# Four-head layer: scores in four row groups and banks, masks added by VectorE, keys in one copy, no loop

## The chip, the cores and the metric

One core of a Trainium2 chip (trn2) runs the kernel. Times are device microseconds of one execution, the median of the runs of a kernel; the profile and its rows come from one profiled execution. The tensor engine is called TensorE or PE, the vector engine VectorE or DVE, the activation engine ScalarE or ACT, the general one GpSimd or POOL.

## The reference, cut to what matters

Four transformer layers follow each other on x of 16 x 256 tokens of 128 features. The change is in the third ("layer 2", counted from 0), whose attention has four heads of 32 features, and a feed-forward part beside it:

```python
q_in = x @ Wq.T
qkv = (q_in @ Wqkv.T + bqkv).reshape(Bs, Ls, 3, Ds)       # q, k, v: G = 4 heads, dh = 32
scores = einsum('blgd,bmgd->bglm', q, k) * scale
h = relu(q_in) @ Wop.T
dx = sigmoid(h @ W2.T + b2) * Ls                          # one reach per token
dx_g = dx[:, None, :, :] + windows[None, :, None, None]   # windows 32, 64, 128, 256
win_mask = where(idx[None, :] < idx[:, None], BIG, dist)
masked = where(win_mask > dx_g, -BIG, scores)
attn = softmax(masked + scores)
out = einsum('bglm,bmgd->blgd', attn, v)
# beside it, on the same normed x
h = silu(x @ w1 * w1_s) * (x @ w2 * w2_s)                 # 512 wide
h = gelu(h @ h1 * h1_s); h = gelu(h @ h2 * h2_s)          # 512 x 512 twice
y = h @ w3 * w3_s
```

Both results are added to x.

## The kernel before, in words

Layer 2 (`layer2`) works in eight passes (`PASSES = 8`) over two sequences each, 512 tokens. Each engine has a hardware loop (`Fori`) of its own over the passes; between them stand semaphores (`sig(...)`), whose values a loop works out in registers. An engine executes its list in order, so the order written in `pe_`, `act_`, `dve_` and `pool_` is the order of the work. Two sequences of a pass are the blocks p = 0 and 1.

TensorE, in this order: the queries' input (bank 4), `up` (the gated first stage of the feed-forward, banks 6, 7 and 0, 1), the reach (bank 5), q, v and k (bank 4 in turn); `mid(0, 0)` and `mid(1, 0)` for the first two chunks; `scores(0)`; the rest of `mid(0..3, 0)`, which is the first 512 x 512 stage in three products per chunk; `turn()`, the transposes of the next pass's normed x into bank 4; `scores(1)`; `turned(0, g)`, the transposes of the softmax weights of block 0, laced with the second 512 x 512 stage `mid(c, 1)`; `values(0)`; `turned(1, g)`; `wide_out`, `values(1)` and the sum in bank 2. Where the columns of a line say 128*128 they are rows and columns of the loaded weights.

`scores(p)` before: three bf16 products of the identity with the masks put the masks into banks 0, 1 and 2 (L1733, L1734), then three f32 products over all 128 rows add the scores (L1736, L1737). For this the keys lie in `kb`, a copy for each head with zeros in the other heads' rows; ScalarE writes the four copies (L1853), and GpSimd has cleared the whole array once.

VectorE, in order: relu (L1959), `gated(c)` (L1949), q's copy, the reach, `split` of h into high and low parts (L1941, L1943, signal `f_h`), `masks(0)`, two more splits, `masks(1)`, `stats` (L1901), `maxima(0)` (L1982, L1983, three reductions with the sign turned), the norm of the next pass, `sums(0)`, the splits of the gelus (signal `f_sp`) for chunks 0 and 1, `maxima(1)`, `turned_out(0, 1)` (L1993, the copies of the transposed weights), splits of chunks 2 and 3, further copies, the final addition (L2012).

ScalarE, in order: q_in's copy (L1840), the reach's exp (L1842), `silu(0..3)` (L1836) with v's copy between, the keys, `exps(0)` (L1860, L1863, eight exps with row sums), four `gelu` (L1869, signal `f_ig`), the copy of the turned x (L1877), `exps(1)`, `head_out(0)` (L1887), four gelus, `head_out(1)`. A function of another table costs an ACT_TABLE_LOAD ahead of it.

GpSimd multiplies the weights by the reciprocal sums (L2028, L2029).

In layer 1, a loopless part of the same kernel, VectorE already adds masks and takes maxima in one instruction (`tensor_tensor_reduce`, L1483 and L1484, shown as CUSTOM_DVE_ANT_0), and ScalarE takes the exps of its result (L1373, L1374). In layer 0 four row groups of TensorE give scores into four banks (L793).

Of the kernel before, what the change touches and what calls it, by code (L numbers as in the profile page):

```python
# [68 lines left out]
def program(nc, ins, out):  # L69
# [3 lines left out]
    with ctx:  # L73
# [1562 lines left out]
        def layer2():  # L1636
# [4 lines left out]
            kb = carve(G2, 512)  # L1641
# [18 lines left out]
            PRE = 8  # L1660
            ORDER = ["in", "q", "v", "k", "t"]
# [6 lines left out]
            MID_BANKS = ((6, 7, 5, 3), (6, 7, 0, 1))  # L1668
# [8 lines left out]
            def pe_(pe):  # L1677
# [10 lines left out]
                pe.wait_ge(pre_k, 2)  # L1688
                pe.wait_ge(pre, 4)
                with pe.Fori(0, PASSES) as i:  # L1690
# [13 lines left out]
                    def mid(c, layer, parts=range(C2)):  # L1704
# [3 lines left out]
                        if parts[0] == 0:  # L1708
                            pe.wait_ge(pre, PRE)
                            if layer == 0 and c == 0:  # L1710
                                pe.wait_ge(f_h.s, f_h.at(i, 1))
                            if layer == 0 and c == 2:
                                pe.wait_ge(ot.s, ot.at(i, -1))
                                pe.wait_ge(d_e.s, d_e.at(i, 0))
                            if layer == 0 and c == 3:
                                pe.wait_ge(t_e.s, t_e.at(i, -1))
                            if layer == 1 and c == 2:
                                pe.wait_ge(s_ex.s, s_ex.at(i, 1))
# [21 lines left out]
                    def turned(p, g):  # L1740
# [7 lines left out]
                        for c, src in enumerate((pr0[p][:, g, 128:256], pr1[p][:, g, :], pr0[p][:, g, 0:128])):  # L1748
                            mm = pe.transpose(PS[(3, 4)[n % 2]][:, c * 128:(c + 1) * 128], src, ident)
                        mm.then_inc(t_f.s, 1)  # L1750

                    def values(p):
                        pe.wait_ge(t_e.s, t_e.at(i, 4 * p + G2 - 1))
                        pe.wait_ge(ot.s, ot.at(i, p - 1))
                        for g in range(G2):
                            r = slice(DH2 * g, DH2 * (g + 1))
                            pe.matmul(PS[5][r, 0:256], v_sb[:, 2 * p + 1, r], pt[g][:, 0:256], start=True, stop=False, skip_group_check=True)
                        for g in range(G2):
                            r = slice(DH2 * g, DH2 * (g + 1))
                            pe.matmul(PS[5][r, 0:128], v_sb[:, 2 * p, r], pt[g][:, 256:384], start=False, stop=True,  # L1760
# [13 lines left out]
                    pe.wait_ge(ot.s, ot.at(i, -1))  # L1774
# [22 lines left out]
                    mid(3, 0)  # L1797
                    pe.wait_ge(ln_x.s, ln_x.at(i, 0))
# [29 lines left out]
            def act_(act):  # L1828
                act.wait_ge(m_f.s, m_f.before(0))
                act.activation(xnT, PS[4][:, :], ACT.Copy).then_inc(m_e.s, 1)  # L1830
                act.wait_ge(pre_k, 2)
                with act.Fori(0, PASSES) as i:
# [18 lines left out]
                    for g in range(G2):  # L1851
                        r = slice(DH2 * g, DH2 * (g + 1))
                        ins_ = act.activation(kb[r, g, :], PS[4][r, :], ACT.Identity, bias=L["bk"][r, :])  # L1853
                    ins_.then_inc(m_e.s, 1)

                    def exps(p):
                        act.wait_ge(s_mx.s, s_mx.at(i, p))
                        act.wait_ge(t_f.s, t_f.at(i, 4 * p + 3 - 8))
                        for g in range(G2):
                            act.activation(pr0[p][:, g, :], PS[g // 2][:, g % 2 * 256:(g % 2 + 1) * 256], ACT.Exp, bias=nmx[:, p, 0, g:g + 1],  # L1860
                                           accum_out=sm[:, p, 0, g:g + 1])
                        for g in range(G2):
                            ins_ = act.activation(pr1[p][:, g, :], PS[2][:, g * 128:(g + 1) * 128], ACT.Exp, bias=nmx[:, p, 1, g:g + 1],  # L1863
# [21 lines left out]
            def head_out(act, i, p):  # L1885
                act.wait_ge(pv.s, pv.at(i, 4 * p + 3))
                act.activation(oT[:, p * 256:(p + 1) * 256], PS[5][:, 0:256], ACT.Identity, bias=L["bv"]).then_inc(ot.s, 1)  # L1887

            def dve_(dve):
# [45 lines left out]
                with dve.Fori(0, PASSES) as i:  # L1935
# [9 lines left out]
                    def gated(c):  # L1945
                        dve.wait_ge(f_s.s, f_s.at(i, c))
# [42 lines left out]
                    def turned_out(*which):  # L1989
                        for n in which:  # L1990
                            dve.wait_ge(t_f.s, t_f.at(i, n))
                            dve.wait_ge(pv.s, pv.at(i, n - G2))
                            dve.tensor_copy(pt[n % G2], PS[(3, 4)[n % 2]][:, 0:384]).then_inc(t_e.s, 1)  # L1993
# [21 lines left out]
            def pool_(pool):  # L2015
                pool.memset(kb, 0.0).then_inc(pre_k, 1)
# [5 lines left out]
                with pool.Fori(0, PASSES) as i:  # L2022
# [139 lines left out]
```

## Time and profile before

| | |
|---|---|
| median of 3 runs | 2264.98 us (2264.29 to 2267.79) |
| the profiled execution | 2265.04 us |
| its span | 2263.2 us |
| the passes of layer 2 | about 1277 to 1699 us of the span |
| PE busy | 2043.8 us |
| DVE busy | 1461.5 us |
| ACT busy | 1159.4 us |
| POOL busy | 895.9 us |

Matmuls are pipelined: one starts before the last has ended, so the distance between starts is the cost of one in a row, and the length printed is longer. In a timeline row the first number is the start, the second the time covered; in brackets is the idle time of that engine before it and what ended it. PEclk is the share of the full TensorE clock that was granted, 1.00 for 2.4 GHz and 0.50 for 1.2 GHz.

### The profile page before, as it was taken

To read this page: it belongs to the slowest core of one execution; us is meant where nothing else is said; L and a number is where in the kernel's file an instruction comes from. 1 tells how busy PE (TensorE), PEld (TensorE's weight loads), DVE (VectorE), ACT (ScalarE), POOL (GpSimd) and SP (SyncE) were. 2 spreads that over 40 slices of the span, in tenths; PEclk is the share of its full clock that TensorE was granted. 3 is DMA by queue.
4 is the path that set the end of the run, shared out by engine and by line. 5 is a ranking of instruction groups with operands and counts; after the bars stand their busy time and mean duration, and the time that the engine had idled before them with its cause. 6 is when DMAs were issued, how large, how long until landed. Compare 5 with 4: busy or idle time off the path is not lost.

```text
span 2263.2 us, 47747 instructions
## 1 busy us (share of the span) xinstructions
PE 2043.8 (90%) x15692; PEld 1546.9 (68%) x15692; DVE 1461.5 (65%) x5301; ACT 1159.4 (51%) x3600; POOL 895.9 (40%) x1416
## 2 busy tenths in 40 slices
PE   5887977399999999999999899999997999999998
PEld 2555644277777777777777566666665777777776
DVE  6999843366666666666666655555556777777776
ACT  3443342155455555555554455555545666666665
POOL 3113255345455444444444411111114545454554
PEclk9887779689999999999999899999998999999999
DMA  6000016600000000000000000000000000000001
GB/s 190 8 1 1 8 34 159 173 2 1 2 2 1 1 2 1 2 2 1 2 2 1 1 0 0 0 0 0 0 0 1 2 2 2 2 2 1 2 1 39
DMA packets 37479, 36.86 MB, mean 16 GB/s; under 512 B 5648, under 2 KB 34448, under 8 KB 36368
## 3 DMA queue, kind: packets, MB, share of 16 engines
q1 hardware_dynamic: 31632, 29.82, 4.2%
q0 software_dynamic: 5632, 4.33, 1.4%
q8 instruction: 116, 1.90, 0.3%
q14 instruction: 99, 0.81, 0.1%
HBM read 23.53 MB, written 10.62 MB: 15 GB/s over the span
## 4 chain that ended last, share of the span: by engine, by line
PE 67%; issue 11%; DVE 8%; ACT 8%; POOL 4%; DMA 1%; DVEq 0%; SPq 0%; another core or an unknown queue 0%; POOLq 0%; ACTq 0%
PE bank L1313 7%; PE bank L1302 6%; PE bank L1241 5%; PE bank L1288 4%; PE bank L1285 4%; PE bank L1335 4%; PE bank L1226 2%; PE bank L1228 2%; PE bank L1227 2%; ACT work L1373 2%; PE bank L1700 2%; PE bank L1722 2%; PE bank L1305 2%; PE bank L1234 2%; PE bank L1724 2%
## 5 line engine op out<-in xcount | busy, mean ns | idle before, releaser
L1596 POOL TENSOR_TENSOR work<-work 128x128 f32<-128x128 f32 (+1 forms) x1048 | 503.6, 512 | 698.5 <-DVE work L1496 698.5
L1373 ACT ACTIVATE work<-work 128x128 f32<-128x128 f32 x524 | 206.7, 395 | 546.0 <-DVE work L1484 546.0
L1491 DVE COPY work<-bank 128x384 f32<-128x384 f32 x520 | 283.6, 550 | 26.5 <-PE bank L1313 11.1
L1374 ACT ACTIVATE work<-work 128x256 f32<-128x256 f32 x524 | 258.6, 493 | 0.0
L1313 PE MATMUL bank<-w_const,work 128*128 128x128 f32 x1560 | 228.9, 283 | 1.0 <-POOL work L1596 1.0
L1484 DVE CUSTOM_DVE_ANT_0 work<-bank,mask 128x256 f32<-128x256 f32 x524 | 220.0, 420 | 0.0
L1313 PEld LDWEIGHTS bank<-w_const,work 128*128 128x128 f32 x1560 | 166.9, 141 | 47.5 <-issue 43.1
L1517 DVE COPY work<-bank 128x512 f32<-128x512 f32 x136 | 93.5, 687 | 158.7 <-PE bank L1236 152.1
L1483 DVE CUSTOM_DVE_ANT_0 work<-bank,mask 128x128 f32<-128x128 f32 x524 | 151.0, 288 | 53.6 <-PE bank L1288 49.1
L1302 PE MATMUL bank<-work 128*64 128x256 f32 x1032 | 171.7, 410 | 4.4 <-DVE work L1517 4.0
L1226 PE MATMUL bank<-l_xn_hi,l_qk_hi 128*128 128x256 f32 x532 | 163.6, 308 | 2.9 <-DVE l_xn_lo L1437 2.8
L1288 PE MATMUL bank<-work 64*128 64x256 f32 x1048 | 163.5, 390 | 0.0
L1392 ACT ACTIVATE work<-bank 128x512 f32<-128x512 f32 x266 | 154.4, 580 | 9.0 <-PE bank L1228 8.4
L1228 PE MATMUL bank<-l_xn_hi,l_qk_lo 128*128 128x256 f32 x532 | 151.3, 284 | 0.0
L1227 PE MATMUL bank<-l_xn_lo,l_qk_hi 128*128 128x256 f32 x532 | 150.7, 283 | 0.0
L1335 PE MATMUL bank<-w_l,work 128*128 128x128 f32 x1024 | 134.8, 275 | 0.0
L1609 POOL TENSOR_TENSOR work<-work 128x512 f32<-128x512 f32 x129 | 134.3, 1041 | 0.0
L1285 PE MATMUL bank<-work 64*128 64x128 f32 x1048 | 133.1, 332 | 0.0
L1335 PEld LDWEIGHTS bank<-w_l,work 128*128 128x128 f32 x1024 | 125.0, 191 | 0.0
L1285 PEld LDWEIGHTS bank<-work 64*128 64x128 f32 x1048 | 81.7, 191 | 62.9 <-issue 49.9
L1496 DVE RECIPROCAL work<-work 128x2 f32<-128x2 f32 x524 | 84.9, 162 | 54.5 <-ACT work L1374 52.4
L1302 PEld LDWEIGHTS bank<-work 128*64 128x64 f32 x1032 | 53.5, 137 | 95.3 <-issue 95.3
(338 smaller groups left out, 4934.2 us busy)
## 6 DMA issues: line engine op xcount, KB each, us to landing
w_l<-in_l SPq DMA_DIRECT2D x1, 3210.5 KB, 10.4
w_l<-in_l SPq DMA_DIRECT2D x2, 1540.0 KB
w_f<-in_f SPq DMA_DIRECT2D x1, 3072.0 KB, 13.9
x_sb<-in_x SPq DMA_DIRECT2D x4, 512.0 KB, 6.0
normed_rows<-work SPq DMA_DIRECT2D x1, 2048.0 KB, 9.3
even_experts<-x_sb SPq DMA_DIRECT2D x8, 256.0 KB, 3.6
residual<-x_sb SPq DMA_DIRECT2D x1, 2048.0 KB, 9.7
qk<-in_qk SPq DMA_DIRECT2D x2, 1024.0 KB
```

The lines of the kernel that those rows point to most:

```text
L1226: pe.matmul(to, qk_hi[:, n, ws], x, start=True, stop=False)
L1228: mm = pe.matmul(to, qk_lo[:, n, ws], x, start=False, stop=True)
L1285: pe.matmul(scored(i, 2 * j + n)[:, Q0], q[r, 0:128], q[r, 256:384], start=True, stop=True, skip_group_check=True)
L1288: pe.matmul(scored(i, 2 * j + n)[:, Q1], q[r, 128:256], q[r, 256:512], start=True, stop=True, skip_group_check=True).then_inc(s_f.s, 1)
L1302: pe.matmul(PS[5][r, 0:256], v[:, 0, h], pt[(2 * j + n) % 4][:, 0:256], start=True, stop=False, skip_group_check=True)
L1313: mm = pe.transpose(PS[2 + g % 2][:, to * 128:(to + 1) * 128], pr[g % 4][:, c * 128:(c + 1) * 128], ident)
L1335: mm = pe.matmul(PS[7][:, t * 128:(t + 1) * 128], h2[u % 2][:, c * 256 + t * 128:c * 256 + (t + 1) * 128], L["down"][:, (2 * e + c) * D:(2 ...
L1373: act.activation(pr[g % 4][:, Q0], pr[g % 4][:, Q0], ACT.Exp, scale=-1.0, bias=nmx[:, g % 4, 0:1], accum_out=sm[:, g % 4, 0:1])
L1374: act.activation(pr[g % 4][:, Q1], pr[g % 4][:, Q1], ACT.Exp, scale=-1.0, bias=nmx[:, g % 4, 1:2], accum_out=sm[:, g % 4, 1:2]).then_inc(s ...
L1484: dve.tensor_tensor_reduce(pr[g % 4][:, Q1], scored(i, g)[:, Q1], mask[:, Q1], -1.0, BIG, ALU.add, ALU.min, nmx[:, g % 4, 1:2]).then_inc(s ...
L1491: dve.tensor_copy(pt[g % 4], PS[2 + g % 2][:, 0:384]).then_inc(s_te.s, 1)
L1596: ins = pool.tensor_tensor(w, w, spread(rc[:, g % 4, q:q + 1], w.shape[1]), ALU.mult)
```

## The change

Scores of a head come from its own 32 rows of `qT` and `kT`, as eight products, four with 256 and four with 128 columns, each head into a bank of its own (0 to 3). The keys are one array `kT` with one copy, and the clearing of the old one is gone. The mask products are gone; VectorE adds the bf16 masks while it takes the maxima, writes the masked scores (with the sign turned) to SBUF, and ScalarE takes the exps from there. The banks are dealt anew: `mid(2, 0)` and `mid(3, 0)` use banks 4 and 5, the turned weights 5 and 4, the values bank 3. The waits follow: `turn()` waits for the third gelu of the stage, since its bank 4 is now read by it; `scores` waits for the maxima of the last block. The four `Fori` are Python loops, so that the eight passes stand one after the other in the program.

```diff
-            MID_BANKS = ((6, 7, 5, 3), (6, 7, 0, 1))
+            MID_BANKS = ((6, 7, 4, 5), (6, 7, 0, 1))
+            TURN_BANKS = (5, 4)
...
-                with pe.Fori(0, PASSES) as i:
+                for i in range(PASSES):
...
                             if layer == 0 and c == 2:
-                                pe.wait_ge(ot.s, ot.at(i, -1))
+                                pe.wait_ge(m_e.s, m_e.at(i, place["k"]))
+                            if layer == 0 and c == 3:
                                 pe.wait_ge(d_e.s, d_e.at(i, 0))
-                            if layer == 0 and c == 3:
                                 pe.wait_ge(t_e.s, t_e.at(i, -1))
                             if layer == 1 and c == 2:
-                                pe.wait_ge(s_ex.s, s_ex.at(i, 1))
+                                pe.wait_ge(s_mx.s, s_mx.at(i, 1))
...
                     def scores(p):
-                        pe.wait_ge(mb_s.s, mb_s.at(i, p))
-                        pe.wait_ge(s_ex.s, s_ex.at(i, p - 1))
-                        pe.wait_ge(o_e.s, o_e.at(i, -1))
-                        for j in range(2):
-                            pe.matmul(PS[j][:, :], ident16[:, :], mb0[p][:, 2 * j:2 * j + 2, :].rearrange("p g k -> p (g k)"), start=True, stop=False)
-                        pe.matmul(PS[2][:, :], ident16[:, :], mb1[p].rearrange("p g k -> p (g k)"), start=True, stop=False)
-                        for j in range(2):
-                            pe.matmul(PS[j][:, :], qT[:, p * 256:p * 256 + 128], kb[:, 2 * j:2 * j + 2, p * 256:(p + 1) * 256], start=False, stop=True)
-                        pe.matmul(PS[2][:, :], qT[:, p * 256 + 128:(p + 1) * 256], kb[:, :, p * 256 + 128:(p + 1) * 256],
-                                  start=False, stop=True).then_inc(s_f.s, 1)
+                        pe.wait_ge(s_mx.s, s_mx.at(i, p - 1))
+                        if p == 0:
+                            pe.wait_ge(dv.s, dv.at(i, GATED_3))
+                            pe.wait_ge(o_e.s, o_e.at(i, -1))
+                            pe.wait_ge(ot.s, ot.at(i, -1))
+                        for g in range(G2):
+                            r = slice(DH2 * g, DH2 * (g + 1))
+                            pe.matmul(PS[g][:, 0:256], qT[r, p * 256:p * 256 + 128], kT[r, p * 256:(p + 1) * 256], start=True, stop=True, skip_group_check=True)
+                        for g in range(G2):
+                            r = slice(DH2 * g, DH2 * (g + 1))
+                            mm = pe.matmul(PS[g][:, 256:384], qT[r, p * 256 + 128:(p + 1) * 256], kT[r, p * 256 + 128:(p + 1) * 256],
+                                           start=True, stop=True, skip_group_check=True)
+                        mm.then_inc(s_f.s, 1)
...
                     mid(3, 0)
+                    pe.wait_ge(f_ig.s, f_ig.at(i, 2))
                     pe.wait_ge(ln_x.s, ln_x.at(i, 0))
                     turn()
                     scores(1)
...
-                    for g in range(G2):
-                        r = slice(DH2 * g, DH2 * (g + 1))
-                        ins_ = act.activation(kb[r, g, :], PS[4][r, :], ACT.Identity, bias=L["bk"][r, :])
-                    ins_.then_inc(m_e.s, 1)
+                    act.activation(kT, PS[4][:, :], ACT.Identity, bias=L["bk"]).then_inc(m_e.s, 1)

                     def exps(p):
                         act.wait_ge(s_mx.s, s_mx.at(i, p))
-                        act.wait_ge(t_f.s, t_f.at(i, 4 * p + 3 - 8))
                         for g in range(G2):
-                            act.activation(pr0[p][:, g, :], PS[g // 2][:, g % 2 * 256:(g % 2 + 1) * 256], ACT.Exp, bias=nmx[:, p, 0, g:g + 1],
+                            act.activation(pr0[p][:, g, :], pr0[p][:, g, :], ACT.Exp, scale=-1.0, bias=nmx[:, p, 0, g:g + 1],
                                            accum_out=sm[:, p, 0, g:g + 1])
-                        for g in range(G2):
-                            ins_ = act.activation(pr1[p][:, g, :], PS[2][:, g * 128:(g + 1) * 128], ACT.Exp, bias=nmx[:, p, 1, g:g + 1],
+                            ins_ = act.activation(pr1[p][:, g, :], pr1[p][:, g, :], ACT.Exp, scale=-1.0, bias=nmx[:, p, 1, g:g + 1],
...
                     def maxima(p):
+                        dve.wait_ge(mb_s.s, mb_s.at(i, p))
                         dve.wait_ge(s_f.s, s_f.at(i, p))
-                        for j in range(2):
-                            dve.tensor_reduce(nmx[:, p, 0, 2 * j:2 * j + 2], PS[j][:, :].rearrange("p (g k) -> p g k", k=256), AX, ALU.max, negate=True)
-                        dve.tensor_reduce(nmx[:, p, 1, :], PS[2][:, :].rearrange("p (g k) -> p g k", k=128), AX, ALU.max, negate=True).then_inc(s_mx.s, 1)
+                        dve.wait_ge(t_f.s, t_f.at(i, 4 * p + 3 - 8))
+                        for g in range(G2):
+                            dve.tensor_tensor_reduce(pr0[p][:, g, :], PS[g][:, 0:256], mb0[p][:, g, :], -1.0, BIG, ALU.add, ALU.min, nmx[:, p, 0, g:g + 1])
+                            ins_ = dve.tensor_tensor_reduce(pr1[p][:, g, :], PS[g][:, 256:384], mb1[p][:, g, :], -1.0, BIG, ALU.add, ALU.min,
+                                                            nmx[:, p, 1, g:g + 1])
+                        ins_.then_inc(s_mx.s, 1)
...
-                pool.memset(kb, 0.0).then_inc(pre_k, 1)
```

## Rows read from the trace of the kernel before

**Rows 1.** The page, busy time: engine, us, share of the span, instructions.

```profile
PE 2043.8 (90%) x15692; PEld 1546.9 (68%) x15692; DVE 1461.5 (65%) x5301; ACT 1159.4 (51%) x3600; POOL 895.9 (40%) x1416
```

**Rows 2.** Windows, one pass: stretch, us, busy (instructions) of PE, PEld, DVE, ACT, POOL, PEclk, DMA.

```profile
1489.89:1542.14 52.25, 51.00 (x253) 34.84 (x253) 28.47 (x71) 27.55 (x60) 6.98 (x5) 1.00 0.00 0
```

**Rows 3.** The chain that ended last, in that pass: shares by line, then start, us, what.

```profile
by line: PE bank L1722 10.7%; PE bank L1700 10.3%; PE bank L1724 10.0%; PE bank L1723 9.9%; PE bank L1767 9.5%; PE bank L1736 6.4%; issue 6.2%; ACT work L1853 3.9%; PE bank L1737 3.2%; PE bank L1825 3.1%; PE bank L1749 2.5%; PE bank L1757 2
...
1505.21 0.60 PE bank L1733 x2
...
1507.75 0.86 PE bank L1737 x2
...
1516.96 0.44 PE bank L1683 x4
...
1520.62 0.67 PE bank L1749 x6
...
1526.05 0.50 PE bank L1722
```

**Rows 4.** Timeline of VectorE in the same pass, around the maxima of both blocks.

```profile
1506.08 0.69 DVE L1943 TENSOR_TENSOR lo_h<-work,hi_h 128x512 fp32r<-128x512 f32 x1
...
1509.53 1.29 DVE L1982 TENSOR_REDUCE work<-bank 128x2 f32<-128x512 f32 x2
...
1511.33 0.37 DVE L1906 BATCH_NORM_AGGREGATE work<-work 128x2 f32<-128x6 f32 x4
...
1521.06 1.28 DVE L1982 TENSOR_REDUCE work<-bank 128x2 f32<-128x512 f32 x2
...
1522.85 1.01 DVE L1993 COPY work<-bank 128x384 f32<-128x384 f32 x2
...
1525.30 0.69 DVE L1943 TENSOR_TENSOR lo_hA<-work,hi_hA 128x512 fp32r<-128x512 f32 x1
```

**Rows 5.** Timeline of ScalarE in the same pass: keys, exps of block 0, gelus.

```profile
1502.12 2.76 ACT L1853 ACTIVATE work<-bank,w_l 32x512 f32<-32x512 f32 x4
1511.51 1.28 ACT L1860 ACT_TABLE_LOAD   x1 [6.62 <-DVE work L1983]
1512.81 0.48 ACT L1860 ACTIVATE work<-bank,work 128x256 f32<-128x256 f32 x1
...
1517.45 2.42 ACT L1869 ACTIVATE work<-bank,w_l 128x512 f32<-128x512 f32 x4
```

**Rows 6.** Timeline of layer 1: masks with maxima, exps, two heads each.

```profile
900.60 0.29 DVE L1483 CUSTOM_DVE_ANT_0 work<-bank,mask 128x128 f32<-128x128 f32 x1
...
901.16 0.29 DVE L1483 CUSTOM_DVE_ANT_0 work<-bank,mask 128x128 f32<-128x128 f32 x1
...
901.28 0.40 ACT L1373 ACTIVATE work<-work 128x128 f32<-128x128 f32 x1 [4.09 <-DVE work L1484]
...
902.17 0.39 ACT L1373 ACTIVATE work<-work 128x128 f32<-128x128 f32 x1
```

**Rows 7.** Timeline of ScalarE at the start of layer 3, which has no loop.

```profile
1718.79 1.28 ACT L1373 ACT_TABLE_LOAD   x1
...
1721.31 0.40 ACT L1373 ACTIVATE work<-work 128x128 f32<-128x128 f32 x1 [1.24 <-DVE work L1484]
```

**Rows 8.** Timeline of TensorE in layer 0: four heads in four row groups.

```profile
267.11 0.79 PE L793 MATMUL bank<-w_l 32*128 32x304 f32 x8
```

**Rows 9.** Windows around pauses of TensorE, columns as in Rows 2.

```profile
1147.98:1151.40 3.42, 3.42 (x27) 2.36 (x28) 2.38 (x12) 0.10 (x1) 1.01 (x2) 1.00 0.00 0
1195.23:1197.60 2.37, 0.01 (x1) 0.01 (x1) 1.01 (x4) 2.31 (x9) 1.89 (x5) 1.00 0.00 0
1197.60:1201.00 3.40, 3.40 (x13) 2.00 (x15) 1.66 (x6) 0.00 (x0) 1.00 (x2) 0.50 0.00 0
1271.29:1275.10 3.81, 0.00 (x1) 0.01 (x1) 2.56 (x15) 0.00 (x0) 2.44 (x2) 0.69 0.00 0
1280.60:1286.20 5.60, 5.60 (x14) 3.39 (x13) 0.00 (x0) 2.63 (x4) 5.60 (x2) 0.50 0.00 0
```

More of the change, by code:

```diff
@@ L1640, in layer2 @@
             xnT, qin, rq, qT = carve(512), carve(512), carve(512), carve(512)
-            kb = carve(G2, 512)
+            kT = carve(512)
             v_sb = carve(4, 128)
@@ L1660, in layer2 @@
             PRE = 8
+            GATED_3 = 8
             ORDER = ["in", "q", "v", "k", "t"]
@@ L1687, in pe_ @@
                 turn()
-                pe.wait_ge(pre_k, 2)
+                pe.wait_ge(pre_k, 1)
                 pe.wait_ge(pre, 4)
-                with pe.Fori(0, PASSES) as i:
+                for i in range(PASSES):
                     def free(n):
@@ L1748, in turned @@
                         for c, src in enumerate((pr0[p][:, g, 128:256], pr1[p][:, g, :], pr0[p][:, g, 0:128])):
-                            mm = pe.transpose(PS[(3, 4)[n % 2]][:, c * 128:(c + 1) * 128], src, ident)
+                            mm = pe.transpose(PS[TURN_BANKS[n % 2]][:, c * 128:(c + 1) * 128], src, ident)
                         mm.then_inc(t_f.s, 1)
@@ L1754, in values @@
                         pe.wait_ge(ot.s, ot.at(i, p - 1))
+                        pe.wait_ge(s_mx.s, s_mx.at(i, 1))
                         for g in range(G2):
                             r = slice(DH2 * g, DH2 * (g + 1))
-                            pe.matmul(PS[5][r, 0:256], v_sb[:, 2 * p + 1, r], pt[g][:, 0:256], start=True, stop=False, skip_group_check=True)
+                            pe.matmul(PS[3][r, 0:256], v_sb[:, 2 * p + 1, r], pt[g][:, 0:256], start=True, stop=False, skip_group_check=True)
                         for g in range(G2):
                             r = slice(DH2 * g, DH2 * (g + 1))
-                            pe.matmul(PS[5][r, 0:128], v_sb[:, 2 * p, r], pt[g][:, 256:384], start=False, stop=True,
+                            pe.matmul(PS[3][r, 0:128], v_sb[:, 2 * p, r], pt[g][:, 256:384], start=False, stop=True,
                                       skip_group_check=True).then_inc(pv.s, 1)
@@ L1773, in pe_ @@
                     pe.wait_ge(rq_s.s, rq_s.at(i, 0))
-                    pe.wait_ge(ot.s, ot.at(i, -1))
                     for t in range(4):
@@ L1830, in act_ @@
                 act.activation(xnT, PS[4][:, :], ACT.Copy).then_inc(m_e.s, 1)
-                act.wait_ge(pre_k, 2)
-                with act.Fori(0, PASSES) as i:
+                act.wait_ge(pre_k, 1)
+                for i in range(PASSES):
                     def silu(c):
@@ L1886, in head_out @@
                 act.wait_ge(pv.s, pv.at(i, 4 * p + 3))
-                act.activation(oT[:, p * 256:(p + 1) * 256], PS[5][:, 0:256], ACT.Identity, bias=L["bv"]).then_inc(ot.s, 1)
+                act.activation(oT[:, p * 256:(p + 1) * 256], PS[3][:, 0:256], ACT.Identity, bias=L["bv"]).then_inc(ot.s, 1)
             def dve_(dve):
@@ L1934, in dve_ @@
                 dve.sem_inc(pre_k, 1)
-                with dve.Fori(0, PASSES) as i:
+                for i in range(PASSES):
                     k[0] = 0
@@ L1945, in gated @@
                     def gated(c):
+                        assert c < 3 or k[0] == GATED_3, k[0]
                         dve.wait_ge(f_s.s, f_s.at(i, c))
@@ L1992, in turned_out @@
                             dve.wait_ge(pv.s, pv.at(i, n - G2))
-                            dve.tensor_copy(pt[n % G2], PS[(3, 4)[n % 2]][:, 0:384]).then_inc(t_e.s, 1)
+                            dve.tensor_copy(pt[n % G2], PS[TURN_BANKS[n % 2]][:, 0:384]).then_inc(t_e.s, 1)
                     maxima(0)
@@ L2021, in pool_ @@
                     pool.tensor_tensor(lo_w[n], L[w], hi_w[n].bitcast(F32), ALU.subtract).then_inc(pre, 1)
-                with pool.Fori(0, PASSES) as i:
+                for i in range(PASSES):
                     for p in range(2):
```

## The prediction

> **What bounds the kernel now.** First the page: TensorE is busy for 90% of the span, VectorE for 65%, ScalarE for 51% [rows 1]. That is a mean over four layers, so I turn to the window of one pass of layer 2: 52.25 us long, TensorE busy for 51.00 of it, VectorE for 28.47, at full clock [rows 2]. Eight passes make 418 us; a tenth of a microsecond in each is 0.8 us in the whole. The chain of that pass runs mostly over TensorE lines, with 6.2% "issue" [rows 3]. So each product that goes looks like a gain. The timelines say otherwise: they show a second chain, over VectorE and ScalarE, almost as long as TensorE's, and the change moves TensorE's work behind it. I name moments by their time in this pass, and give the new time of the same moment, with the start of the pass kept where it is.
>
> **TensorE up to the end of the first 512 x 512 stage.** Before, `scores(0)` begins at 1505.21 and its last f32 product ends its turn at 1507.75 + 0.86 = 1508.61: 3.40 us. It began late by 0.3 us, since the four copies of the keys end at 1502.12 + 2.76 = 1504.88 [rows 3, 5]. `scores(1)` takes from 1516.96 + 0.44 = 1517.40 to 1520.62: 3.22 us [rows 3]. The f32 products alone are 3 x 0.86 = 2.58 us, the masks the rest. Afterwards the masks are gone, and the f32 columns are the same in number, 4 x 384 against 3 x 512, but in four row groups. The nearest row has four row groups of 304 columns each in 0.79 us [rows 8], in which one after the other they would need 4 x 304/512 x 0.86 = 2.04 us: the groups do run beside each other. The 256 columns then take about 0.65 us and the 128, where loading weights weighs more, about 0.45: I take 1.1 us. Bounds: 0.8 us if both halves together cost what the row shows, 2.58 us if nothing overlaps.
>
> The Trainium skill, page "TensorE: Matmul & The Clock Gate", section "Measured speedup vs the span model", gives 3.07 times for four row groups of 512 columns; 2.58/3.07 is an estimate of 0.84 us, which agrees with the row's ratio of 2.04/0.79 = 2.6 within the shorter products, and the sum would be about 2 us lower by it.
>
> The keys are now one copy of 0.7 us instead of 2.76, so `scores(0)` starts as soon as TensorE comes to it, at 1504.9, and ends at 1506.0. The rest of the stage is 36 products from 1508.61 to 1516.96, 0.232 us each [rows 3]. Its last split must be there for most of them: it ends at 1506.08 + 0.69 = 1506.77 [rows 4], so the stage ends at about 1506.8 + 33 x 0.232 = 1514.5. TensorE has gained 2.5 us here. It can use them only if nothing holds it next.
>
> **The new wait ahead of the transposes.** `turn()` now writes bank 4, which `mid(2, 0)` fills, and waits for the third gelu. Before, bank 4 was free, and TensorE went through `turn()` and `scores(1)` while ScalarE worked on. When does the third gelu end? `maxima(0)` stands at its place in VectorE's list: VectorE is without a pause from 1506.08 to 1511.33 and comes to the maxima at 1509.53 whatever TensorE does [rows 4]. Scores that are there 2.6 us sooner bring nothing. The three reductions took 1511.33 - 1509.53 = 1.80 us; the new form takes 901.16 - 900.60 = 0.56 us for a head's 128 and 256 columns in layer 1 [rows 6], so 4 x 0.56 = 2.24 us, and the maxima are ready at 1511.8 instead of 1511.4. ScalarE then loaded its table only behind that wait, at 1511.51, and began the exps at 1512.81 [rows 5]. Its exps had two waits, the load stood between them; with one wait left, the load goes ahead of it, as in layer 3, where it runs at 1718.79 and the exp starts at 1721.31 when VectorE releases it [rows 7]. So the exps begin at 1511.9. A pair takes 902.17 - 901.28 = 0.89 us from SBUF [rows 6], four 3.56, and end at 1515.5, where they ended at 1516.1. The load for the gelus follows (1.28), the gelus start at 1516.8 instead of 1517.45, and the third of four (2.42 in all, 0.58 apart) ends at 1518.7. TensorE, finished at 1514.5, stands still for 4.2 us, and restarts with `turn()` 1.75 us later than before. The gain is spent.
>
> **What follows.** At full clock `turn()` 0.44 and `scores(1)` 1.1 end at 1520.3. VectorE's splits of the first two gelus come 0.6 us sooner with the gelus, so `maxima(1)` starts at 1520.45 instead of 1521.06, takes 2.24 instead of 1.79, and the copies and two splits behind it (1522.85 to 1525.30 + 0.69 = 1525.99, 3.1 us [rows 4]) end at 1525.8. TensorE's product that waits for the last split started at 1526.05 [rows 3], and would now start 0.25 us sooner. From there TensorE is the bound up to the next pass, and nothing of it changes.
>
> **The clock.** A pause of 4.2 us is new here. What the trace shows of pauses: layer 1 has 16 of 2.37 us; after 11 of them the granted clock was 0.50 for 3.4 us, as at 1197.60, after 5 it stayed at 1.00, as at 1147.98; after the 3.81 us before layer 2 it had dropped too, and was still 0.50 during 5.6 us of unbroken work up to 1286.2 [rows 9]. A pause of 4.2 us is longer than all of these, so I take it that the clock drops in each pass, and stays at 1.2 GHz for some 5 us of the work behind it. Then `turn()` takes 0.88 us and `scores(1)` 2.2, ending at 1521.85; `maxima(1)` ends at 1524.1, the last split at 1527.25. TensorE meanwhile does two `turned` (0.65, now 1.3, to 1523.1), 12 products (2.8 us, 3.1 with the slow start, to 1526.2), two `turned` (1526.9) and three products, and starts the last group at 1527.55 against 1526.05: 1.5 us later. With 3.4 us at the lower clock it is 1.2, with 7 us 2.4, and if the clock only drops after TensorE has started again, 0.75.
>
> The Trainium skill, same page, section "HAM oscillation — how this bites in real kernels", speaks against this change: a pause that comes back with every tile lets the clock fall in every tile. By this rule all eight passes pay, which is what I took from rows 9; by the rows alone 11 of 16 short pauses did.
>
> **The loop.** Straight code turns register arithmetic at waits into constants. The chain's "issue" is 6.2% of the 54 us that this view covers, 3.35 us [rows 3], and holds at least one table load (1.28, the length in rows 5), the one ahead of the silus, since TensorE then waits for them. So at most 2 us of a pass is register work on the path, at least nothing; most "issue" pieces lie between instructions that follow each other on an engine, so I take 0.15. Straight code must be fetched; layers 1 and 3 have none of this as a visible stall, so nothing, but up to 0.5 us a pass can't be excluded. The cleared `kb` (once, GpSimd, ahead of the loop) gives 0.4 us. Banks 3 and 5 for the values and waits on `ot` and `gated(3)` in `scores(0)` come free well before 1504.9 (the values of the last pass, the last silu ahead of the keys' copy at 1502.12 [rows 5]): nothing; if a bank were late, TensorE would pay it whole, at this place.
>
> **The sum.** 8 x (1.5 - 0.15) - 0.4 = +10.4 us. Against the profiled execution's 2265.04 (0.06 above the median) that is 2275.4; I say 2275.
>
> **The rivals.** (a) The lower clock does not come, or costs nothing: 8 x (-0.25 - 0.15) - 0.4 = -3.6, so 2261: no change. For it: 5 of 16 pauses left the clock alone; against it: all those were 2.37 us. 15%. (b) The row groups don't overlap as f32, or `scores(1)` costs nearly the sequential 2.58 us: at the lower clock it ends 3 us later, +3.4 a pass, 2290. Against it stands rows 8. 8%. (c) The clock stays low for 7 us or more, or fetching adds to it: +2.4 a pass and more, 2283 to 2287. 10%. (d) The other side: VectorE's chain isn't the wait that counts, since TensorE meets no pause. That needs the third gelu by 1514.5, 4.2 us sooner than I derive; then both scores' savings stand, 2.5 + 2.1 = 4.6 us a pass less up to 0.1 for the maxima, 8 x 4.5 = 36, so 2229. Part of it, or 1 us of register work a pass on top of (a) (8 us less, 2255), makes the middle. For it: TensorE is 90% of the chain; against it: VectorE's unbroken row up to 1511.33. It decides at a pause of zero, and pays in the measure in which the pause falls short of 2.5 us. 17%. The forecast itself has 50%.
>
> **Chances and range.** Measurement tells this kernel from no change at about 0.2%, 4.5 us. Slower: 50 + 8 + 10 less 1 for a small forecast case, 67%. Same: 15 and 1, 16%. Faster: 17%. The range leaves out the far part of (d) and the end of (b): 2254 to 2292. The likeliest case alone would be 2269 to 2284.
>
> **What would show it.** In the profile after: TensorE idle for about 4 us ahead of the transposes, put down to ScalarE's gelu; a granted clock of 0.50 behind it; four score products starting within 0.1 us; a table load ahead of the maxima's end; maxima of 2.2 us; passes of 53.6 us. Wrong would be: no pause there (then d), full clock after it (then a), or score products one after the other (then b).

## The result, and the profile after

The changed kernel takes 2273.44 us (median of 7 runs, 2269.78 to 2275.7) against 2266.64 us (7 runs, 2264.29 to 2267.79) for the kernel before beside it. The ratio is 1.0032, with an interval of 1.0023 to 1.0042: slower by about 7 us. The prediction was 2275.0, slower by 0.44%. The profiled execution has a span of 2270.9 us against 2263.2.

The page's line of busy times answers [rows 1]:

```profile
PE 2016.8 (89%) x15804; PEld 1541.8 (68%) x15804; DVE 1467.9 (65%) x5509; ACT 1145.9 (50%) x3575; POOL 893.9 (39%) x1415
```

TensorE is busy 27.0 us less than before, and the span is 7.7 us longer. The busiest engine did lose work; it was not given the time. The pass that answers [rows 2] shows where the time is. First comes the whole pass, then its pause, the stretch behind the pause, and the work after that (columns as in [rows 2]):

```profile
1495.05:1548.93 53.88, 49.33 (x269) 35.56 (x267) 29.52 (x97) 26.22 (x57) 6.97 (x5) 0.94 0.00 1
1519.86:1523.72 3.86, 0.08 (x1) 0.00 (x0) 1.26 (x3) 3.83 (x9) 2.81 (x2) 0.99 0.00 0
1523.73:1530.30 6.57, 6.49 (x32) 5.26 (x33) 5.42 (x23) 3.76 (x9) 0.26 (x1) 0.50 0.01 4
1530.40:1534.00 3.60, 3.60 (x20) 3.03 (x19) 2.75 (x6) 2.24 (x12) 0.47 (x1) 1.00 0.00 0
```

TensorE is busy for 49.33 us of the pass instead of 51.00, and the pass is 1.63 us longer. For 3.86 us TensorE does nothing (the one product in that row is the tail of the last), while ScalarE is busy throughout. Behind that, 6.57 us run at a granted clock of 0.50, which is 1.2 GHz; after them it is back at 1.00. The view of waits puts a name and a count to the pause (line of the engine, releaser, then total, number, longest):

```profile
PE bank L1685 <- ACT work L1870: 31.0, 8, 3.9
```

Line 1685 is `turn()`, line 1870 the gelu: eight passes, 31.0 us in all. The timeline of TensorE in the same pass answers [rows 3]:

```profile
1510.06 0.71 PE L1738 MATMUL bank<-work 32*128 32x256 f32 x8
1510.60 0.40 PE L1741 MATMUL bank<-work 32*128 32x128 f32 x8
1510.98 0.50 PE L1724 MATMUL bank<-hi_h,hi_h 128*128 128x512 f32 x1
...
1523.81 1.11 PE L1685 MATMUL bank<-w_const,work 128*128 128x128 f32 x4 [3.87 <-ACT work L1870]
1524.85 1.24 PE L1738 MATMUL bank<-work 32*128 32x256 f32 x8
1525.87 0.65 PE L1741 MATMUL bank<-work 32*128 32x128 f32 x8
1526.45 1.54 PE L1754 MATMUL bank<-w_const,work 128*128 128x128 f32 x6
```

The eight matmuls of a row stand for four heads, each product being recorded as two. At full clock `scores(0)` holds TensorE from 1510.06 to 1510.98, for 0.92 us where it was 3.40; at the lower clock `scores(1)` holds it from 1524.85 to 1526.45, for 1.60 us where it was 3.22. The chain now leaves TensorE inside the pass (its shares by line, over 1495 to 1550 us):

```profile
by line: PE bank L1724 7.8%; PE bank L1726 7.5%; PE bank L1725 7.4%; PE bank L1773 7.3%; PE bank L1702 6.8%; PE bank L1754 5.1%; DVE work L1956 3.5%; ACT work L1870 3.4%; ACT work L1862 3.3%; issue 3.3%; PE bank L1777 3.2%; DVE work L1957 3
```

VectorE's masks (lines 1956 and 1957), ScalarE's exps (1862) and gelus (1870) have come into it, and "issue" has fallen from 6.2% to 3.3%. The timelines of VectorE and ScalarE, which answer [rows 4, 5], show that second chain:

```profile
1514.64 0.43 DVE L1986 CUSTOM_DVE_ANT_0 work<-bank,work 128x256 f32<-128x256 f32 x1
...
1516.86 0.38 DVE L1907 BATCH_NORM_AGGREGATE work<-work 128x2 f32<-128x6 f32 x4
...
1526.68 0.42 DVE L1986 CUSTOM_DVE_ANT_0 work<-bank,work 128x256 f32<-128x256 f32 x1 [1.08 <-PE bank L1741]
```

```profile
1507.41 0.69 ACT L1857 ACTIVATE work<-bank,w_l 128x512 f32<-128x512 f32 x1 [0.17 <-PE bank L1794]
1508.12 1.28 ACT L1862 ACT_TABLE_LOAD   x1
1516.98 0.51 ACT L1862 ACTIVATE work<-work 128x256 f32<-128x256 f32 x1 [7.58 <-DVE work L1987]
...
1521.91 2.42 ACT L1870 ACTIVATE work<-bank,w_l 128x512 f32<-128x512 f32 x4
```

To compare moments I take as zero the first matmul of the pass in the timeline, 1495.05 here. Before it was 1489.72; the 1489.89 of [rows 2] comes from the view of the chain, which counts a matmul only from the end of the one ahead. The two rows of before, from its timeline:

```profile
1489.72 1.02 PE L1771 MATMUL bank<-work,w_l 128*128 128x512 f32 x2
...
1516.80 0.60 PE L1683 MATMUL bank<-w_const,work 128*128 128x128 f32 x4
```

`maxima(0)` begins at 19.59 us, and before it began at 19.81: the scores of block 0, ready 3.7 us before that, wait for their place in VectorE's list. The exps begin at 21.93 (before 23.09), the gelus at 26.86 (before 27.73), and `turn()`, which waits for the third gelu, at 28.76 (before 27.08, when it waited for none).

From pass to pass the length varies: 53.69, 52.82, 53.38, 53.88, 52.52 and 53.60 us for the six steady ones between the first and the last, 53.32 on average, where all of before are 52.22 to 52.28. The clock is low behind the pause in all eight, but not for the same time. Two windows behind the restart of the pass of 52.82 us, with the columns of the fence above:

```profile
1417.60:1420.90 3.30, 3.29 (x24) 2.59 (x25) 2.33 (x8) 2.41 (x3) 0.18 (x1) 0.53 0.00 0
...
1421.30:1424.00 2.70, 2.70 (x14) 2.19 (x13) 2.67 (x16) 1.32 (x6) 0.00 (x0) 1.00 0.00 0
```

Here it is back at 1.00 within 3.7 us, and so it is in the last pass; in the first and in the pass of 52.52 us it is back within about 4 us (0.95 and 0.96 on average over the second window). In the other four the clock was low for 5.4 to 6.6 us, an estimate from the means of such windows. The first pass takes 56.17 us against 56.00. It is not like the others: the clock is already low when it begins, here for some 9 us and in the profile of before for as long.

### The profile page after: what moved, and what is told of

It reads as the page before. It is cut to its first block, busy times and chain, and to the rows that moved or that the text cites. A ratio compares the mean times of both kernels' runs of the same rounds, so it can differ in the third digit from the quotient of the medians.

```text
span 2270.9 us, 47502 instructions
## 1 busy us (share of the span) xinstructions
PE 2016.8 (89%) x15804; PEld 1541.8 (68%) x15804; DVE 1467.9 (65%) x5509; ACT 1145.9 (50%) x3575; POOL 893.9 (39%) x1415
## 4 chain that ended last, share of the span: by engine, by line
PE 62%; DVE 11%; ACT 11%; issue 10%; POOL 3%; DMA 2%; another core or an unknown queue 0%; SPq 0%; POOLq 0%; DVEq 0%; ACTq 0%
PE bank L1313 7%; PE bank L1302 6%; PE bank L1241 5%; PE bank L1288 4%; PE bank L1285 4%; PE bank L1335 4%; ACT work L1373 2%; PE bank L1226 2%; PE bank L1228 2%; PE bank L1227 2%; PE bank L1305 2%; PE bank L1234 2%; ACT work L1374 2%; PE bank L1702 2%; PE bank L1773 1%
## 5 line engine op out<-in xcount | busy, mean ns | idle before, releaser
L1483 DVE CUSTOM_DVE_ANT_0 work<-bank,mask 128x128 f32<-128x128 f32 x524 | 150.8, 288 | 53.4 <-PE bank L1288 49.1
```

## The experiments

Nine kernels were run in three sets; in each set the kernel before ran on the same chip, with medians of 2243.91, 2262.82 and 2266.84 us. These differ by 1%, so only ratios and the lengths of passes are compared between sets. "Pass" is the steady pass, measured like the ones above; the kernel before has one profile only, from beside the changed kernel. That passes can be compared between sets is shown by the changed kernel, with 53.32 and 53.33 us in two of them.

| kernel | kernel before, us | median, us | ratio (95%) | pass, us |
|---|---|---|---|---|
| before | | 2266.64 | 1 | 52.25 |
| after | 2266.64 | 2273.44 | 1.0032 (1.0023 to 1.0042) | 53.32 |
| a0_after | 2262.82 | 2270.72 | 1.0032 (1.0021 to 1.0043) | 53.33 |
| e1_fill | 2243.91 | 2240.93 | 0.9978 (0.9967 to 0.9988) | 51.79 |
| e7_before_wait | 2243.91 | 2264.40 | 1.0089 (1.0073 to 1.0106) | 54.5 |
| e5_before_noloop | 2243.91 | 2237.18 | 0.9967 (0.9953 to 0.9981) | 51.51 |
| e9_onewait | 2266.84 | 2265.31 | 0.9989 (0.9979 to 0.9999) | 51.80 |
| e3_early | 2243.91 | 2225.24 | 0.9907 (0.9891 to 0.9924) | 49.85 |
| e4_noloop_early | 2262.82 | 2257.27 | 0.9967 (0.9953 to 0.998) | 51.5 |
| e2_deal | 2262.82 | 2260.63 | 0.9991 (0.9983 to 1.0) | 51.8 to 52.2 |
| e8_copies | 2262.82 | 2236.32 | 0.9883 (0.9869 to 0.9897) | 48.87 |

The theory was that of the prediction: `turn()` waits for the third gelu, the pause lets the clock fall, and the lower clock costs more than the pause and the scores leave as a gain. The rivals were that the loss comes from the straight code, from the slower maxima or from the dealing of the banks itself.

### The changed kernel once more

> The changed kernel itself, beside the others on one chip: a ratio of 1.003 to the kernel before, and in each of the eight passes a pause of 3.87 us with the clock at 0.50 behind it.

Nothing is edited. It measured 1.0032 again, with steady passes of 53.83, 52.63, 53.52, 52.96, 53.19 and 53.84 us, and the same pause ahead of `turn()` with the low clock behind it in all eight. Both the result and the spread of the passes come back. The first pass does not: it takes 54.45 us here instead of 56.17, and at its start the clock is low for about 4 us instead of 9.

### The pause filled with products

```diff
                     mid(3, 0)
+                    pe.wait_ge(s_mx.s, s_mx.at(i, 0))
+                    for _ in range(15):
+                        pe.matmul(PS[3][:, :], hi_w[0][:, 0:128], hi_w[0][:, 0:512], start=True, stop=True)
                     pe.wait_ge(f_ig.s, f_ig.at(i, 2))
```

The 15 products fill the pause and nothing reads them; everything that the reference wants is still computed, and the wait for the gelu stays.

> The changed kernel with 15 products of constants (0.23 us each, 3.5 us together) put into the pause of 3.87 us that TensorE has ahead of turn(); nothing waits for their result. Theory (the lower clock behind the pause is what costs): the granted clock stays 1.00, scores(1) end 0.75 to 0.85 us after they start instead of 1.6, each pass is shorter by 1.0 to 1.2 us, the whole by 8 to 10 us against the changed kernel's 2273.4: 2264 to 2266, level with the kernel before. Rival (the wait for the third gelu itself is the whole loss, the clock only a sign of it): 2272 to 2275, as without the products. Second rival (the clock drops all the same): 2273 and a clock of 0.50 in the windows.

The ratio went from 1.0032 to 0.9978, which is 12 us of the whole, by adding work. The timeline of TensorE:

```profile
1493.95 3.59 PE L1805 MATMUL bank<-hi_h 128*128 128x512 f32 x15
1497.99 0.66 PE L1685 MATMUL bank<-w_const,work 128*128 128x128 f32 x4 [0.45 <-ACT work L1873]
1498.58 0.71 PE L1738 MATMUL bank<-work 32*128 32x256 f32 x8
...
1499.44 0.88 PE L1754 MATMUL bank<-w_const,work 128*128 128x128 f32 x6
```

and the windows of the same pass: all of it, the filled stretch, the work behind it.

```profile
1469.23:1521.02 51.79, 50.27 (x284) 36.01 (x282) 29.33 (x97) 26.24 (x57) 6.98 (x5) 1.00 0.00 1
...
1493.95:1497.54 3.59, 3.59 (x16) 2.63 (x14) 0.90 (x3) 3.56 (x8) 2.45 (x2) 1.00 0.00 0
1497.99:1503.00 5.01, 5.01 (x39) 4.12 (x40) 4.98 (x22) 3.37 (x8) 0.18 (x1) 1.00 0.01 2
```

`turn()` starts 28.76 us into the pass, the very moment as after: the wait is unchanged. Only the clock differs, 1.00 instead of 0.50, and `scores(1)` takes 0.86 us (1498.58 to 1499.44) instead of 1.60. All steady passes are 51.77 to 51.82, so the lower clock costs 53.32 - 51.79 = 1.53 us a pass, and the spread goes with it. That is more than the 1.0 to 1.2 us expected. Of all the runs this one shows the clock's part: the wait is the same, the work is more, and the pass is shorter. It also says that without the lower clock the whole change would be a gain of about 0.2%.

### The wait alone, in the kernel before

```diff
                     mid(3, 0)
+                    pe.wait_ge(f_ig.s, f_ig.at(i, 2))
                     pe.wait_ge(ln_x.s, ln_x.at(i, 0))
                     turn()
```

> The kernel before with one wait more, that of the change: turn() waits for the third gelu. Theory: TensorE comes to it at the same time as before and waits 2.35 us (from 1516.96 to 1519.3 in the pass that was read); scores(1), 3.2 us long here, then end at 1523.0, the VectorE chain behind them is later by 1.95 us, the whole by 8 x 1.95 = 16 us at full clock, and by up to 32 us where the clock drops behind the pauses: 2282 to 2298. Rival (slack elsewhere in the pass takes the wait up): within 5 us of the kernel before.

It costs 2.3 us a pass (1.95 had been expected at full clock) and 20 us in all, the slowest kernel of the study. The row of `turn()` in its timeline, and the window of a pass:

```profile
1506.74 0.65 PE L1683 MATMUL bank<-w_const,work 128*128 128x128 f32 x4 [2.46 <-ACT work L1870]
```

```profile
1477.05:1531.58 54.53, 50.78 (x252) 34.75 (x253) 28.57 (x71) 27.63 (x60) 6.98 (x5) 1.00 0.00 0
```

Here the pause is 2.46 us and the clock stayed at 1.00 in all passes but one, of 55.92 us. So the same wait costs by the pause itself where the old scores leave TensorE no slack, and by the clock where the new scores have given it slack and the pause is 1.4 us longer.

### The loops made straight code, in the kernel before

```diff
-                with pe.Fori(0, PASSES) as i:
+                for i in range(PASSES):
```

and the same for the loops of ScalarE, VectorE and GpSimd.

> The kernel before with the four hardware loops of layer 2 written out, nothing else. Theory: register work at waits is worth 0.15 to 0.25 us a pass, 1 to 2 us in all: 2264 to 2265.5, no change that can be told. Rival: 1 to 2 us a pass are register work: 2250 to 2258. Rival on the other side: fetching the longer program costs up to 0.5 us a pass: 2270.

The ratio is 0.9967, some 7 us of the whole, and a steady pass is 0.74 us shorter (51.51). Of what was expected, the theory's one or two microseconds for the whole were too small, and the rival's one or two microseconds for each pass too large. The timeline of ScalarE explains a part:

```profile
1477.25 1.28 ACT L1860 ACT_TABLE_LOAD   x1
...
1483.61 0.48 ACT L1860 ACTIVATE work<-bank,work 128x256 f32<-128x256 f32 x1 [5.08 <-DVE work L1983]
```

The table load went ahead of the wait, although the exps of this kernel still have both their waits. So the reason given for it, that only one wait is left, can't be the whole of it, and the next run separates the two.

### One wait for the exps, loops kept

```diff
                     def exps(p):
                         act.wait_ge(s_mx.s, s_mx.at(i, p))
-                        act.wait_ge(t_f.s, t_f.at(i, 4 * p + 3 - 8))
...
                     def maxima(p):
+                        dve.wait_ge(t_f.s, t_f.at(i, 4 * p + 3 - 8))
                         dve.wait_ge(s_f.s, s_f.at(i, p))
```

> The kernel before, loops kept, with the second wait of exps (for the transposes of the last block) moved from ScalarE to VectorE's maxima, as the change has it. Theory of the prediction (the table load stood behind the wait for the maxima because exps had two waits): the load goes ahead, the gelus come 1.3 us sooner, maxima(1) starts when scores(1) are done instead of 0.6 us behind them, a pass is 0.5 to 0.6 us shorter, ratio 0.998. Rival (in a loop a wait on a register stands as an instruction of its own ahead of the load, whatever their number, and only the straight code moved it): passes of 52.25 us, ratio 1.000, the load still 1.3 us ahead of the exps.

```profile
1508.77 1.28 ACT L1859 ACT_TABLE_LOAD   x1
...
1515.42 0.48 ACT L1859 ACTIVATE work<-bank,work 128x256 f32<-128x256 f32 x1 [5.36 <-DVE work L1983]
```

With the loops kept and one wait, the load goes ahead too, and a pass is 51.80 us: 0.45 less than before. So either step suffices: one wait in a loop, or two waits in straight code. What they have in common I can only argue: in a loop a wait's value comes from a register, and a second such wait is likely an instruction of its own, behind which the load then stands. Straight code saves 0.45 by the load and 51.80 - 51.51 = 0.29 besides.

### The maxima called sooner in VectorE's list

```diff
                     split(h0, hi_0, lo_0, 3, f_h)
-                    masks(1)
                     tile = 4 * i + 4
-                    stats(i, tile)
...
                     maxima(0)
+                    stats(i, tile)
                     moments()
                     variance(i)
+                    masks(1)
```

This is the changed kernel with nothing but the order of VectorE's work changed.

> The changed kernel with another order in VectorE's list: maxima(0) right behind the splits, ahead of stats and masks(1), which follow it. Theory (the scores are ready 2.7 us before VectorE comes to them, and everything up to the third gelu hangs on that place): exps, gelus and so turn() come 2.6 us sooner, the pause shrinks from 3.87 to about 1.2 us, the clock stays up, the last split of the gelus is 3.5 to 4.5 us sooner, and the whole takes 8 x 4 to 5 us less than 2273.4: 2233 to 2242. Rival (TensorE's own work bounds a pass near the 52.3 us of the kernel before): no lower than 2262. Second rival (the masks of block 1 or the norm come too late and become the new wait): 2255 to 2265.

```profile
1460.48:1510.28 49.80, 47.18 (x269) 33.12 (x267) 29.96 (x97) 26.25 (x57) 7.04 (x5) 1.00 0.00 1
```

```profile
1486.50 0.66 PE L1685 MATMUL bank<-w_const,work 128*128 128x128 f32 x4 [1.13 <-ACT work L1870]
```

(The window of a pass, then the timeline's row of `turn()`.) The maxima no longer stand behind block 1's masks and the statistics. The pause shrinks from 3.87 to 1.13 us, the clock stays at 1.00, and a pass is 49.85 us, 3.47 less than after. Of this the clock is 1.53, the price that the filled pause showed, and 51.79 - 49.85 = 1.94 is the earlier release. In ratio it is 1.0032 to 0.9907, some 28 us; 4 to 5 us a pass had been expected. The prediction's statement that "scores that are there 2.6 us sooner bring nothing" holds for the order as changed, and only for it.

### The same order, without the new scores

The edit of the last experiment, made to the kernel before with its loops as straight code.

> The kernel before without loops, and with maxima(0) ahead of stats and masks(1), the order that took 28 us from the changed kernel. Theory (in the old form TensorE sets scores(1), so VectorE's order is worth nothing there, and only the new form of the scores makes it pay): passes of 51.5 us as without loops alone, ratio 0.9967 +- 0.001. Rival (the order alone is the gain, the new scores have no part in it): passes below 50.5 us, ratio below 0.994.

```profile
1487.92:1539.40 51.48, 50.73 (x255) 34.84 (x254) 29.56 (x71) 27.61 (x60) 7.04 (x5) 1.00 0.00 1
```

The pass is as long as without the new order (51.5), and so is the ratio (0.9967 both). The order is worth nothing while TensorE's own work sets the moment of `scores(1)`, and 1.94 us a pass, or 3.47 with the clock, once it does not. The new scores, with the single copy of the keys and the new banks that belong to them, are worth, compared in this order and at full clock in the steady passes, 51.5 - 49.85 = 1.65 us a pass.

### Bank 4 left to the transposes

```diff
-            MID_BANKS = ((6, 7, 4, 5), (6, 7, 0, 1))
+            MID_BANKS = ((6, 7, 0, 5), (6, 7, 0, 1))
...
                             if layer == 0 and c == 2:
-                                pe.wait_ge(m_e.s, m_e.at(i, place["k"]))
+                                pe.wait_ge(s_mx.s, s_mx.at(i, 0))
...
-                    pe.wait_ge(f_ig.s, f_ig.at(i, 2))
+                    pe.wait_ge(m_e.s, m_e.at(i, place["k"]))
                     pe.wait_ge(ln_x.s, ln_x.at(i, 0))
                     turn()
+                    pe.wait_ge(f_ig.s, f_ig.at(i, 2))
                     scores(1)
```

> The changed kernel with the banks dealt otherwise: mid(2, 0) goes to bank 0, so it waits for maxima(0), turn() waits for nothing, and scores(1) waits for the third gelu. The same wait is thus split: about 2.7 us ahead of mid(2, 0), about 0.8 ahead of scores(1), which no turn() stands before. Theory: with no drop of the clock a pass is 51.8 us, as with the pause filled; where the clock drops behind the 2.7 us it falls on mid(2, 0) and mid(3, 0) and costs 0.9 us: 51.8 to 52.7 a pass, ratio 0.997 to 1.000, better than the changed kernel's 1.003. Rival (what counts is the time until the third gelu, not the clock): turn() alone is saved, 0.44 us a pass, ratio 1.001 to 1.002.

```profile
1508.66 0.47 PE L1724 MATMUL bank<-hi_h,hi_h 128*128 128x512 f32 x1 [2.65 <-issue]
...
1515.88 0.60 PE L1685 MATMUL bank<-w_const,work 128*128 128x128 f32 x4
1516.41 0.71 PE L1738 MATMUL bank<-work 32*128 32x256 f32 x8
```

```profile
1506.01:1508.66 2.65, 0.00 (x0) 0.03 (x1) 2.62 (x21) 0.06 (x1) 0.00 (x0) 1.00 0.00 0
1508.66:1515.88 7.22, 7.22 (x24) 5.68 (x25) 3.28 (x11) 6.68 (x20) 4.09 (x3) 0.76 0.01 2
```

The wait has not gone, it has moved: `mid(2, 0)` now writes the bank of the scores and stands still for 2.65 us. The row puts that down to no engine ("issue"); by the edit it waits for `maxima(0)`, which end at 1508.56, and VectorE is busy for 2.62 of the 2.65 us. `turn()` then runs on without a pause. In the passes where the clock stays up, what is left of the wait stands ahead of `scores(1)`, as in this row:

```profile
1463.65 0.71 PE L1738 MATMUL bank<-work 32*128 32x256 f32 x8 [0.53 <-ACT work L1871]
```
Six passes are 51.94, 51.82, 51.78, 52.19, 52.20 and 51.81 us: behind a pause of 2.65 us the clock falls in four passes of the eight (0.76 on average over the 7.22 us here) and not in the others. The ratio is 0.9991, between after and the filled kernel. Passes without the drop are no faster than the filled kernel's, since both wait for the same maxima: not the deal of the banks but VectorE's place for `maxima(0)` holds the time.

### Two copies of the values moved to ScalarE

On top of the earlier maxima:

```diff
                     act.activation(xnT, PS[4][:, :], ACT.Copy).then_inc(m_e.s, 1)
+                    for n in range(2):
+                        act.wait_ge(t_f.s, t_f.at(i, n))
+                        act.wait_ge(pv.s, pv.at(i, n - G2))
+                        act.activation(pt[n % G2], PS[TURN_BANKS[n % 2]][:, 0:384], ACT.Copy).then_inc(t_e.s, 1)
                     exps(1)
...
                             maxima(1)
-                            turned_out(0, 1)
...
+                    dve.wait_ge(t_e.s, t_e.at(i, 1))
                     turned_out(2, 3)
```

> The reordered kernel (ratio 0.9907, passes of 49.85 us) with the first two copies of turned weights on ScalarE, which idles there for 3.5 us, instead of VectorE. Theory (the row of VectorE from maxima(1) to the last split is the bound of that stretch, 4.7 us of it): 0.93 us a pass less, 48.9 us, ratio 0.987 to 0.988. Rival (TensorE's own work bounds it): less than 0.3 us a pass, ratio above 0.9895.

```profile
1499.65 0.87 ACT L1882 ACTIVATE work<-bank 128x384 f32<-128x384 f32 x2 [0.75 <-PE bank L1754]
1500.54 1.28 ACT L1862 ACT_TABLE_LOAD   x1
...
1502.38 0.51 ACT L1862 ACTIVATE work<-work 128x256 f32<-128x256 f32 x1 [0.56 <-DVE work L1989]
```

The copies take 0.87 us of ScalarE, which was waiting for TensorE and, behind them, for VectorE's maxima anyway. A pass is 48.87 us, 0.98 less, the ratio 0.9883. This is the fastest kernel of the study: 1.2% below the kernel before and 1.5% below the changed one.

## Why the prediction was right, step by step

- **The scores.** `scores(0)` took 0.92 us where 1.1 was estimated, `scores(1)` 0.86 us at full clock and 1.60 at half for the 1.1 and 2.2. The row with four row groups of 304 columns [rows 8] was the better guide; I had added too much for loading weights. The row groups do work beside each other: 1536 columns in 0.92 us, where 2.58 us stood for as many one after the other, so rival (b) is out. The single starts, which it named as its sign, are not shown by the view.
- **The pause.** Predicted 4.2 us, from 1514.5 to 1518.7, which is 24.8 to 29.0 us into the pass; measured 3.86 to 3.88 us in all eight passes, from 24.81 to 28.76 in the one shown. Its start was right, and its end, the third gelu, came 0.2 us sooner than predicted. The links between were right (maxima 2.24 us both); what moved is their beginning. The prediction left `maxima(0)` at 19.81 us, and it begins at 19.59. In e5_before_noloop, where only the loops are gone, it begins at 19.57, so the 0.2 us come with the straight code.
- **The table load** went ahead of the maxima as predicted, at 1508.12. The reason given was incomplete: one wait suffices (e9_onewait), but straight code alone does too (e5_before_noloop).
- **The clock.** It fell behind the pause in every pass, so rival (a) is out, and it is the sign of the result: 51.79 us with the pause filled, 53.32 with it open. The term was 1.75 us (from -0.25 to +1.5), measured 1.53. The size varies as the prediction's bounds did: in the profile after, short stretches make passes of 52.5 to 52.8 us, and those of 5.4 to 6.6 us make 53.4 to 53.9. Against the 51.79 that is about 0.9 and 1.9 us, where I had counted 1.45 for 3.4 us and 2.65 for 7. Rival (c)'s long stretch was thus nearly there in four passes of six, but at a smaller price, since `scores(1)` at half clock was 0.6 us shorter than I had it.
- **The rest at full clock.** Predicted 52.25 - 0.25 - 0.15 = 51.85, measured 51.79. The agreement has two misses in it that cancel. Straight code with its table load was worth 0.74 us, where I had only 0.15 for the register work; the register part alone is about 0.3. And what else changed lost 51.79 - 51.51 = 0.28 us, where I had it gaining: `maxima(1)` takes 2.24 us instead of 1.79, and the earlier exps and gelus are already in the 0.74 that the table load is part of.
- **The middle of rival (d).** The other side would have needed the gelu 4.2 us earlier; e3_early gives it 2.7 of them. There the pause falls to 1.13 us and a pass to 49.85, some 2.4 us below before, where (d) had 4.5 for no pause at all. The direction was right. That its size was too large is likely: VectorE's work bounds a part of that pass, as the 0.98 us show that e8_copies takes off it, but a pause of zero was not run.
- **The sum.** The four passes with the long stretch are on average 53.64 us, 1.39 more than before, where 1.35 had been predicted for each. The term that was off is the number of them: the three others that can be measured, the first among them, cost 0.17, 0.57 and 0.27, or 0.34 on average, and the last pass has a short stretch too. 4 x 1.39 + 4 x 0.34 - 0.4 = 6.5 us, against about 7 measured and 10.4 predicted. The prediction had taken one length of the low clock for all passes, though the rows it rested on [rows 9] held both a short and a long one. Two parts of this sum are not firm. The first pass is alike in the two profiles because the clock happened to be low at its start for 9 us in both; in a0_after it was 1.7 us shorter, so the closeness of the sum is in part luck. And no run shows the 0.4 us for the clearing of `kb`: the passes began 1.95 us later in the profile after than before, and 6.2 us sooner in a0_after than in after.

The Trainium skill, page "TensorE: Matmul & The Clock Gate", section "HAM oscillation — how this bites in real kernels", says that such a pause brings the clock down once for every tile, and this case agrees: eight pauses of 3.87 us, eight falls. The Trainium skill, page "TensorEngine Tiling (Array Packing)", section "PSUM Bottleneck", warns that once row groups have made the products short, emptying the banks may come to bound the work, and advises using ScalarE and VectorE both for it. This case agrees: e3_early, with VectorE emptying the scores' banks sooner, won 1.94 us of a pass (the clock apart), and e8_copies, with two of the copies out of the banks given to ScalarE, 0.98 us.

What stays open: why the clock stays low for some 3.5 us in some passes and 5.4 to 6.6 in others of the same kernel, and the cause I argued for the place of the table load. The slower maxima were not run by themselves either. All that the change altered besides the loops and the clock lost 0.28 us a pass in the order as changed, and their share in it is argued.

## What to carry to other kernels

When an edit makes the busiest engine faster, follow the next chain to the place where it meets that engine, before counting the gain: here 4.8 us less of score work on TensorE in each pass (at full clock) gave a pause and no gain, and only another order of VectorE's list made 1.65 us of it real. A pause of TensorE costs more than its length if the clock falls behind it; a run that fills the pause with idle products tells the two apart in one step. And an order that was worth nothing before an edit may be what the edit needs, so reorder after it, not before.

## What the runs showed of the hardware

- Pauses of 3.87 us lowered the clock in 16 of 16 passes (after and a0_after), those of 2.65 us in 4 of 8 (e2_deal), those of about 2.46 us in 1 of 8 (e7_before_wait), those of 1.13 us in none of 8 (e3_early). In layer 1 it was 11 of 16 at 2.37 us [rows 9], so the length of the pause alone does not decide it.
- Four f32 products in four row groups, 256 and 128 columns for each head, hold TensorE for 0.86 to 0.92 us in all at full clock, and for 1.60 us at half. Over all 128 rows, one after the other, as many columns took 3 x 0.86 = 2.58.
- VectorE's addition of a mask with a maximum, from a bank and SBUF, comes every 0.35 us for 128 x 256 and every 0.21 us for 128 x 128 (starts at 1514.64, 1514.99, 1515.20), as in layer 1.
- The hardware loops cost the pass of the kernel before, 52 us long, 0.74 us (e5_before_noloop), of which 0.45 is a table load that stands behind a wait instead of ahead of it (e9_onewait).
